# First norm's rows moved to ScalarE, weight transposes moved behind the angles, two mix blocks interleaved

## The reference

```python
x = x + attn_a(layernorm(x))     # "mix": one attention matrix for all sequences and heads
x = x + ffn(layernorm(x))        # eight experts, each takes its top 256 tokens of a sequence
x = x + attn_b(layernorm(x))     # causal attention, 16 heads
x = x + ffn(layernorm(x))

def attn_a(x):                                   # heads of width 16
    m = xh.mean(axis=(0, 1))                     # mean over sequences and heads: 1024 x 16
    angle = clip(m @ m.T, -pi, pi)               # 1024 x 1024
    attn = softmax(sin(angle * 0.5) ** 2)
    return einsum('ij,bhjd->bhid', attn, xh)
```

## Time and profile before

| what | us |
|---|---|
| median of three runs | 2227.13 |
| the profiled execution | 2232.77 |
| its span in the profile | 2231.0 |
| TensorE busy (96% of the span) | 2145.5 |
| VectorE busy (66%) | 1464.9 |
| GpSimd busy (62%) | 1386.4 |
| ScalarE busy (45%) | 1002.0 |

### The profile page before, as it was taken

The page is one execution under the profiler, slowest core; times in us unless marked ns, Lnnn a source line. Parts: engine busy times, 40 slices in busy tenths (PEclk is TensorE's granted clock), DMA queues, the critical chain, the costliest instruction groups (busy, mean ns, idle before and its releaser), DMA issues.

```text
span 2231.0 us, 34077 instructions
## 1 busy us (share of the span) xinstructions
PE 2145.5 (96%) x12130; PEld 1594.9 (71%) x12130; DVE 1464.9 (66%) x3340; ACT 1002.0 (45%) x1903; POOL 1386.4 (62%) x1250
## 2 busy tenths in 40 slices
PE   6998899999999999999999999999999899999997
PEld 4545788889876666766657666567666588899997
DVE  5365598676757667466774577874876646975553
ACT  4312453454445555345554355542554425434443
POOL 6313676677547776466674576664677846777774
PEclk8999999999999999999999999999999999999999
DMA  4533554565432212222322231221221244545552
GB/s 132 168 111 100 134 131 110 137 159 126 114 86 67 58 32 74 67 56 69 77 58 58 66 86 48 58 67 58 67 77 30 67 133 119 141 111 139 133 144 29
DMA packets 145048, 206.04 MB, mean 92 GB/s; under 512 B 19432, under 2 KB 112112, under 8 KB 144880
## 3 DMA queue, kind: packets, MB, share of 16 engines
q1 hardware_dynamic: 120304, 170.30, 25.6%
q0 software_dynamic: 24576, 33.57, 9.0%
HBM read 130.03 MB, written 39.85 MB: 76 GB/s over the span
## 4 chain that ended last, share of the span: by engine, by line
PE 73%; DVE 8%; POOL 4%; issue 3%; ACT 2%; DMA 1%; SPq 0%; another core or an unknown queue 0%; POOLq 0%; DVEq 0%; ACTq 0%
PE psum L1303 12%; PE psum L1324 11%; PE psum L1450 11%; PE psum L1352 7%; PE psum L1415 7%; PE psum L1431 6%; PE psum L1475 5%; PE psum L1366 4%; PE psum L1380 3%; PE psum L1460 3%; POOL t_acc L2408 2%; DVE f_hlo L2147 1%; DVE f_hhi L2145 1%; PE psum L1271 1%; PE psum L1393 1%
## 5 line engine op out<-in xcount | busy, mean ns | idle before, releaser
L1718 ACT ACTIVATE t_p<-psum 128x512 f32<-128x512 f32 (+3 forms) x768 | 323.8, 492 | 293.8 <-PE psum L1431 284.2
L2408 POOL TENSOR_TENSOR t_acc<-t_acc,t_p 128x1024 f32<-128x1024 f32 (+3 forms) x256 | 417.6, 1631 | 14.2 <-ACT t_p L1718 0.5
L2327 POOL TENSOR_TENSOR f_wlo<-f_wst,f_whi 128x256 fp32r<-128x256 f32 x256 | 222.1, 927 | 152.7 <-ACT f_whi L1651 152.7
L1324 PE MATMUL psum<-f_whi,f_hhi 128*128 128x256 f32 x1024 | 294.9, 288 | 6.6 <-DVE f_hlo L2147 6.6
L1450 PE MATMUL psum<-t_p,t_v 128*64 128x512 f32 (+3 forms) x1536 | 288.8, 496 | 7.4 <-POOL t_p L2388 7.4
L1324 PE MATMUL psum<-f_whi,f_hlo 128*128 128x256 f32 x1024 | 289.4, 283 | 0.0
L1324 PE MATMUL psum<-f_wlo,f_hhi 128*128 128x256 f32 x1024 | 289.2, 282 | 0.0
L2145 DVE CAST f_hhi<-f_h 128x512 fp32r<-128x512 f32 x256 | 142.0, 555 | 211.2 <-ACT f_h L1669 174.2
L1669 ACT ACTIVATE f_h<-psum 128x512 f32<-128x512 f32 x256 | 153.2, 599 | 278.5 <-PE psum L1303 250.0
L1415 PE MATMUL psum<-t_qa,t_ka 128*128 128x512 f32 (+3 forms) x768 | 222.1, 369 | 1.8 <-DVE t_mx L2193 0.7
L2408 POOL TENSOR_TENSOR t_acc<-t_p 128x768 f32<-128x768 f32 x64 | 134.6, 2104 | 135.2 <-PE psum L1460 131.9
(11 more groups left out here) (290 smaller groups left out, 4411.4 us busy)
## 6 DMA issues: line engine op xcount, KB each, us to landing
f_wst<-in_L_ffn_w SPq DMA_DIRECT2D x64, 1024.0 KB
t_ka<-t_ka SPq DMA_DIRECT2D x64, 256.0 KB, 3.2
t_qb<-t_qa SPq DMA_DIRECT2D x64, 256.0 KB, 3.9
t_wk<-wkT SPq DMA_DIRECT2D x32, 256.0 KB, 4.0
t_wq<-wqT SPq DMA_DIRECT2D x32, 256.0 KB, 4.0
t_wv<-wvT SPq DMA_DIRECT2D x16, 512.0 KB, 5.0
normal<-f_xy SPq DMA_DIRECT2D x5, 1024.0 KB, 10.3
a_x<-in_L_attn_a_x SPq DMA_DIRECT2D x4, 1024.0 KB, 7.8
```

What stands on the lines that cost most here:

```text
L1324: m = pe.matmul(out, h[:, js], w[:, f, :], start=(f == 0 and a == 0 and j % 2 == 0), stop=(f == FT - 1 and a == 2), skip_group_check=True)
L1718: act.activation(p[:, i, q0:], k.bank[bank][:, q0:], ACT.Exp, scale=1.0 / float(np.sqrt(k.DH))).then_inc(k.drained[bank], 1)
L2327: m = pool.tensor_tensor(t["wlo"][n % 2][:, i, ks], t["wst"][:, i, ks], t["whi"][n % 2][:, i, ks].bitcast(F32), ALU.subtract)
L2408: pool.tensor_tensor(acc[:, :, q0:], (p0 if kt == 1 else acc)[:, :, q0:], p[:, :, q0:], ALU.add).then_inc(k.p_acc, 1)
```

## The change

ScalarE runs a small activation among the constants, which brings its function table in ahead of the first barrier. In the first norm ScalarE writes seven of eight rows of the first three sequences and GpSimd the eighth; of the last sequence ScalarE writes rows 0, 2 and 4, VectorE 1, 3, 5 and 6 and GpSimd 7. VectorE makes the shift of a sequence inside the statistics of the next, after six of eight. The selection matrix is built behind all statistics. The weight blocks of tensor 0 stand behind the mean and behind the second angle, those of tensors 1 and 2 all behind the angles, with other banks, and VectorE copies out the latter eight. The angles use six banks in place of four, and the first of them wait for only one half of mT. The last three squares stand behind the copies of tensor 1. The products of the first and the second mix block alternate, j by j, and the transposes of the first block's normalized rows come right behind them.

```diff
@@ Kernel
+        self.DVE_ROWS = 1, 3, 5, 6
...
-        firsts = [(step, b) for b in range(B) for step in ("stats", "aggr", "eps")]
+        firsts = []
         for b in range(B):
-            n = firsts.index(("eps", min(b + 1, B - 1))) + 1
-            while n < len(firsts) and firsts[n][0] in ("shift", "row"):
-                n += 1
-            firsts[n:n] = [("shift", b), ("row", b, self.NBLK - 1)]
-        self.d_first = Marks(s("dve_first_norm"), *firsts)
+            firsts += [("shift", b - 1)] * (b > 0) + [("stats", b), ("aggr", b), ("eps", b)]
+        last = [("shift", B - 1)] + [("row", n) for n in self.DVE_ROWS]
+        self.d_first = Marks(s("dve_first_norm"), *firsts, *last)
@@ Program.stage_a
-        for b in range(k.B + 1):
-            if b < k.B:
-                self.first_stats(b)
-            if b:
-                self.first_rows_of(b - 1)
-                if b == k.B:
-                    weights(0)
-                    self.nat_load(2, nat)
-                self.head_sums(b - 1)
+        for b in range(k.B):
+            self.first_stats(b)
+            self.first_rows_of(b)
+            self.head_sums(b)
+        self.selection()
+        self.last_rows()
         self.mean()
+        self.weight_block(0, 0, 0, nat)
+        self.weight_block(0, 0, 1, nat)
         for n in range(k.NBLK):
             self.angle(n)
+            if n == 1:
+                self.weight_block(0, 1, 0, nat)
+                self.weight_block(0, 1, 1, nat)
+                self.nat_load(2, nat)
             self.sine(n)
-            if n % 2:
-                self.weight_block(1, n // 4, n // 2 % 2, nat)
-        for n in range(k.NBLK):
             self.square(n)
+        weights(1)
+        for n in range(k.NSQ, k.NBLK):
+            self.late_square(n)
         weights(2)
...
         for i in range(k.NBLK):
-            for j in range(k.NBLK):
+            for j in range(k.NBLK if i != 1 else 0):
                 self.mix_product(0, i, j)
+                if i == 0:
+                    self.mix_product(0, 1, j)
             if i:
                 self.mixed_transpose(i - 1, t)
@@ TensorE
-        b = self.take(("wT", i, ct, c), 6 + c)
+        b = self.take(("wT", i, ct, c), (6, 7, 6, 7, 6, 7, 1, 2, 3, 4, 5, 7)[4 * i + 2 * ct + c])
...
-            b = self.take(("angle", n, c), 2 + (2 * n + c) % 4)
+            b = self.take(("angle", n, c), (2 + 2 * n + c) % 6)
             self.wait_drained(("mT", 0))
-            self.wait_drained(("mT", 1))
+            if c or n >= k.NBLK // 2:
+                self.wait_drained(("mT", 1))
@@ ScalarE
+    def constants(self):
+
+        k, act = self.k, self.e
+        self.wait_ge(k.p_const, 5)
+        act.activation(k.msum[:, 0:1], k.minus_half[:, 0:1], ACT.Identity)
+
...
         self.wait_ge(k.d_first.sem, k.d_first.at(0, ("shift", b)))
-        for n in range(0, k.NBLK, 2):
+        for n in range(k.NBLK - 1):
+            if b == k.B - 1 and n in k.DVE_ROWS:
+                continue
             act.activation(k.ay[:, n, b, :], k.ax[:, b, n, :], ACT.Identity,
...
     def weight_block(self, i, ct, c, nat):
-        if i == 2:
+        if i:
             return
@@ VectorE
         for n in range(nb):
+            if b and n == 6:
+                self.shift(b - 1)
             s = dve.bn_stats(k.a_stats[:, b, n, :], k.ax[:, b, n, :])
...
-        if b == 0:
-            dve.memset(k.sel[:], 0.0).then_inc(k.d_sel, 1)
...
-    def first_rows_of(self, b):
+
+    def shift(self, b):
+        k, dve, nb = self.k, self.e, self.k.NBLK
         self.wait_ge(k.p_first, b + 1)
         dve.scalar_tensor_tensor(out=k.a_rstd[:, b, nb:2 * nb], in0=k.a_mv[:, b, :, 0], scalar=-1.0,
-                                 in1=k.a_rstd[:, b, 0:nb], op0=ALU.mult, op1=ALU.mult).then_inc(sem, 1)
-        dve.tensor_scalar(k.ay[:, nb - 1, b, :], k.ax[:, b, nb - 1, :], k.a_mv[:, b, nb - 1, 0:1],
-                          k.a_rstd[:, b, nb - 1:nb], ALU.subtract, ALU.mult).then_inc(sem, 1)
+                                 in1=k.a_rstd[:, b, 0:nb], op0=ALU.mult, op1=ALU.mult).then_inc(k.d_first.sem, 1)
...
+    def last_rows(self):
+        k, dve, b = self.k, self.e, self.k.B - 1
+        self.shift(b)
+        for n in k.DVE_ROWS:
+            dve.tensor_scalar(k.ay[:, n, b, :], k.ax[:, b, n, :], k.a_mv[:, b, n, 0:1], k.a_rstd[:, b, n:n + 1],
+                              ALU.subtract, ALU.mult).then_inc(k.d_first.sem, 1)
...
     def weight_block(self, i, ct, c, nat):
-        if i < 2:
+        if not i:
             return
@@ GpSimd.first_stats
         self.wait_ge(k.p_first, b + 1)
-        for n in range(1, nb - 1, 2):
-            pool.tensor_scalar(k.ay[:, n, b, :], k.ax[:, b, n, :], k.a_mv[:, b, n, 0:1], k.a_rstd[:, b, n:n + 1],
-                               ALU.subtract, ALU.mult).then_inc(k.p_rows, 1)
+        n = nb - 1
+        pool.tensor_scalar(k.ay[:, n, b, :], k.ax[:, b, n, :], k.a_mv[:, b, n, 0:1], k.a_rstd[:, b, n:n + 1],
+                           ALU.subtract, ALU.mult).then_inc(k.p_rows, 1)
```

More of the change, by code:

```diff
@@ L411 @@
     mix_load = first_stats = first_rows_of = head_sums = mean = angle = sine = square = skip
+    selection = last_rows = late_square = skip
     mix_exp = mix_rden = mix_product = mix_residual = skip
@@ L1091, in head_sums @@
                 if n == k.NBLK - 1:
-                    self.wait_ge(k.d_first.sem, k.d_first.at(0, ("row", b, n)))
-                elif n % 2:
-                    self.wait_ge(k.p_rows, (k.NBLK // 2 - 1) * b + n // 2 + 1)
+                    self.wait_ge(k.p_rows, b + 1)
+                elif b < k.B - 1:
+                    self.wait_ge(k.a_first, (k.NBLK - 1) * b + n + 1)
+                elif n in k.DVE_ROWS:
+                    self.wait_ge(k.d_first.sem, k.d_first.at(0, ("row", n)))
                 else:
-                    self.wait_ge(k.a_first, k.NBLK // 2 * b + n // 2 + 1)
+                    self.wait_ge(k.a_first, (k.NBLK - 1) * b + n // 2 + 1)
                 for h in range(k.DT):
@@ L1836, in first_stats, with selection @@
         dve.tensor_scalar(k.a_rstd[:, b, 0:nb], k.a_mv[:, b, :, 1], EPS, None, ALU.add).then_inc(sem, 1)
-        if b == 0:
-            dve.memset(k.sel[:], 0.0).then_inc(k.d_sel, 1)
[L1839 to L1842, removed]
-    def first_rows_of(self, b):
-        k, dve = self.k, self.e
-        nb, sem = k.NBLK, k.d_first.sem
+    def shift(self, b):
+        k, dve, nb = self.k, self.e, self.k.NBLK
         self.wait_ge(k.p_first, b + 1)
         dve.scalar_tensor_tensor(out=k.a_rstd[:, b, nb:2 * nb], in0=k.a_mv[:, b, :, 0], scalar=-1.0,
-                                 in1=k.a_rstd[:, b, 0:nb], op0=ALU.mult, op1=ALU.mult).then_inc(sem, 1)
-        dve.tensor_scalar(k.ay[:, nb - 1, b, :], k.ax[:, b, nb - 1, :], k.a_mv[:, b, nb - 1, 0:1],
-                          k.a_rstd[:, b, nb - 1:nb], ALU.subtract, ALU.mult).then_inc(sem, 1)
+                                 in1=k.a_rstd[:, b, 0:nb], op0=ALU.mult, op1=ALU.mult).then_inc(k.d_first.sem, 1)
+    def selection(self):
+        k, dve = self.k, self.e
+        dve.memset(k.sel[:], 0.0).then_inc(k.d_sel, 1)
+        self.wait_ge(k.d_sel, 1)
+        for g in range(4):
+            dve.tensor_reduce(k.sel[:, 32 * g:32 * g + k.DK], k.ident[:].rearrange("p (g d) -> p d g", d=k.DK),
+                              AX.X, ALU.add).then_inc(k.d_sel, 1)
+    def last_rows(self):
[4 more added lines that the diff above has]
+                              ALU.subtract, ALU.mult).then_inc(k.d_first.sem, 1)
     def mean(self):
@@ L1866, in angle, with late_square @@
                               ALU.max).then_inc(k.drained[b], 1)
-    def square(self, n):
+    def late_square(self, n):
         k, dve = self.k, self.e
-        if n < k.NSQ:
-            return
         self.wait_ge(k.a_sin, n + 1)
```

## The result

The changed kernel took 2221.56 us in the median (seven runs, 2219.5 to 2222.29), the kernel before 2227.16 us beside it (seven runs, 2226.24 to 2232.42). The ratio on record is 0.9961 with a 95% interval from 0.9952 to 0.997, 3 to 5 per thousand faster. It is not the quotient of the two medians, which is 0.9975, just outside that interval. A second set on another chip, five runs against nine, gave 2225.64 against 2233.32 us, 0.9962 (0.9948 to 0.9976; the medians' quotient is 0.9966). The forecast was 2220.7 us. The profiled execution took 2221.76 us over a span of 2220.0.

What follows compares the result with a forecast made beforehand. TensorE, without idle time from 62 us, was taken as the bound: 7.0 us gained at the third mix block, less a 0.6 us wait, is -6.4 us, giving 2220.7 us from the median 2227.13; range 2216.5 to 2225.5.

Steps and rivals of the forecast that it cites:

- Its own signs: Prediction wrong if mix starts near 47 at full clock, gap missing, or third block to gathered rows' transposes not kept.
- First norm: Head sums start at 12.8 instead of 17.19, TensorE's pace ends the stage; mean products at 29.4 against 35.88, 6.5 us gained.
- Angles and weights: Angles from 32.45, then eight weight blocks in a row on TensorE; mix starts at 49.4 instead of 59.47.
- I take the same half rate: Assumed TensorE's clock stays at 0.50 through angles and weight transposes, 32 to 49 us, as before.
- rival B: Clock is up during the weight blocks; exponentials limit the mix start to 47.5; -9.7 us in all; 20 in 100.
- Side by side: First two mix blocks end together, so TensorE waits about 2.8 us for rows; third block at 68.2 against 75.23.
- rival C: The 2.8 us gap behind the mix pair lowers the clock, 1.8 us lost; -4.6 us in all; 20 in 100.
- The second wait: TensorE waits 0.6 us more for the second block's rows, whose power stands behind GpSimd's weight subtraction.
- The sum: All steps together: -6.4 us, 2220.7 us from the median; held for 45 in 100.
- Behind the front: Front: time up to the gathered rows' transposes. Claim: TensorE reaching the third mix block earlier moves all the rest equally.

Runs made afterwards that it cites:

- the part alone: Only the first norm's part of the change, on the kernel before (weights, banks and mix order as before): 2225.64 us, ratio 0.9991.
- second look: The changed kernel, unaltered, run again on another chip: 2225.64 us, ratio 0.9962.
- the blocks in turn: The changed kernel with its first two mix blocks one after the other again: 2218.68 us, ratio 0.9956; once more on another chip 2223.27 us, 0.9947.
- the weights alone: The kernel before with only the moved weight blocks, their banks, six angle banks and VectorE's copies; first norm and mix order as before: 2222.37 us, ratio 0.9976.
- the gap was filled: The changed kernel with 12 unread identity products on TensorE ahead of the first block's row transposes: 2226.68 us, ratio 0.9966.
- the weight split later: The changed kernel with first-block row transposes inside the third block and the first weight tensor's rounding, subtraction and store behind the second mixed block: 2223.7 us, 0.9956.
- products ahead: The changed kernel, first two mix blocks one after the other, with unread identity products before the first head sum: 28 gave 2224.58 us (0.9955), 20 gave 2223.15 us (0.9953).

## Why the prediction was right, and where it wasn't

- **Its own signs.** It called itself wrong if the mix started near 47 at full clock, and that happened. It also wanted the distance from the third block to the gathered rows' transposes kept; it grew from 119.58 to 121.39 us. The size of the change came out; of the steps that lead to it, those on the clock did not.
- **First norm.** First head sum forecast for 12.8, measured 12.92 and 13.02; mean products for 29.4, measured 28.62 and 29.78; first angle for 32.45, measured 31.49 and 32.66. TensorE's own pace as the bound is confirmed by the part alone (4.5 us at the mean products, where four weight blocks still stand in the way) and by rows that end at 24.4. The working took 4.8 us for the 22 slow instructions, where its row has 4.5. How long the slow pace lasts changes from one execution to the next: it ended near 16 us in the changed kernel, near 18 in its second look and near 19 with the blocks in turn, so most of the 1.0 us that the first angle came ahead of its forecast is chance.
- **Angles and weights.** From the first clip to the start of the first exponential it was 12.6 us, about as worked (12.8). But "I take the same half rate" for the eight blocks failed. In the changed kernel the clock was at half rate only from 39 to 43 us; it rose near 43, and in the weights alone near 51, each time while nothing but transposes ran. So the mix started at 46.56 and 47.73 instead of 49.4, limited by the exponentials, and its first sixteen products took 13.97 us instead of 15.5. This was rival B; its start for the mix was 47.5. Of the Trainium skill's rule (page "TensorE: Matmul & The Clock Gate", Part 4, PE-mode transpose), that transposes don't count as work for the clock as products do, these runs show no sign: in a row they raised it.
- **Side by side.** The gap was forecast with 2.8 us and measured with 2.76, for the reason given (VectorE's and ScalarE's rows behind one product of cover). That the clock would fall in it was rival C, held for one in five; it fell in all three looks at kernels with this gap unfilled (8.49, 8.73 and 8.73 us for the third block), and not when the gap was filled. That cost 1.5 to 1.7 us.
- **The second wait,** 0.6 us, did not occur, because the slow third block covered it. It was there, 0.34 us, when the clock stayed up.
- **The sum.** Forecast -6.4 us; the front lost 9.43 us in the profiled pair. By its terms, B gained 1.9 us more between first angle and mix (15.1 us instead of 16.95) and 1.5 in the first sixteen products, the first angle came 1.0 earlier than forecast, the second wait was missing (0.6), and C took 1.5 back: -9.9, against 9.43 measured. Of the 0.5 between them, 0.3 lies in two later waits of TensorE, each for VectorE: 1.19 instead of 0.95 us ahead of 165.27, and 2.67 instead of 2.57 ahead of 185.38. The medians moved by 5.6 and 7.7 us, the ratios say 8.7 and 8.5 us, their intervals together 5 to 12. That 2220.7 lay so close to 2221.56 is partly luck: two steps about the clock were wrong, in opposite directions, and what stands behind the front came on top.
- **Behind the front.** "Should move all of the rest by as much" holds only within the scatter. Span less front was from 2031.4 to 2036.2 us for the same instructions in the profiles around the first comparison, and 2036.8 to 2042.3 in those of the other two chips. TensorE ran there at half rate for 30 to 45 us in each, at places that came and went between executions. That is not all of the scatter: the kernel before had 32 us of it in 2036.2, the first norm alone 31 in 2031.4. In nine of the twelve comparisons the medians gained 2 to 4 us less than the front (first norm alone: 4.9 and 2.2 us), in the others between 0.7 less and 1.3 more. The fronts rest on one execution each, though, and that of the kernel before on the first chip was over 5 us above its median. Whether an earlier front systematically costs something later, or these are a few medians of a scattered time, is open; no run here separates it.

The best ratios measured are those of the changed kernel with its first two mix blocks in turn, 0.9956 and 0.9947. The variants with the weight split later and with products ahead (0.9953 to 0.9956) can't be told from it.

## What to carry to other kernels

Two accumulations interleaved finish together, so the chain behind the first loses the cover that the second gave it; do it only if it saves more waiting for inputs than the part of that chain which stays uncovered, here 1.2 us against 2.8. Price an idle stretch of TensorE with the half rate behind it too: 2.8 us of gap cost 1.5 to 1.7 us more. And when a step is moved to close a gap, follow its part on every engine's queue: one transposition moved by five products made TensorE wait for a copy, behind a row, behind a power, behind a subtraction.

## What the runs showed of the hardware

TensorE's clock rose while it did nothing but weight transposes (near 43 us, 0.50 to 0.99), though the stretch from 42 to 62 us of the kernel before, with the same transposes spread between other work and 90% busy, stayed at 0.50. An idle stretch of 2.76 us brought it down in three of three traces, and one of 3.99 us in a fourth; stretches of 1.17 and 1.19 us left it at 1.00. The first head sums ran at about half pace while the profile named clock 1.00, and ran faster once other products had gone ahead of them (14.83 instead of 15.91 us). The same kernel took 2227.8 us on one chip and 2233.3 and 2234.4 us on two others, a difference as large as the whole effect of this change.
